# Attention: the maxima subtracted on strips of 32 rows with the four banks by turns, or on all 128 rows bank by bank

## The chip, the cores and the metric

One core of a Trainium2 chip runs the whole program. The metric is the device time of one execution in microseconds, as the median of the runs.

## The reference

The reference is one decoder block on x of 32 sequences x 128 tokens x 256: a selective scan, a cross attention with a context of the same shape, and a mixture of experts, each added to its input and followed by a normalisation without gain. The change touches the attention alone, cut to what matters:

```python
Q = query @ Wq.T; K = key @ Wk.T; V = value @ Wv.T
Q = _layernorm(Q, ln_gamma, ln_beta)      # over all 256, then 16 heads of 16
K = _layernorm(K, ln_gamma, ln_beta)
scores = jnp.einsum('bhqd,bhkd->bhqk', Q, K) / np.sqrt(D_K)
attn = jax.nn.softmax(scores, axis=-1)
context = jnp.einsum('bhqk,bhkd->bhqd', attn, V)
return context @ Wo.T
x = _layernorm(x + attention, axis=-1)
```

## The kernel before, in words

The program has five stages, each a block that all engines leave together: the scan, the attention, the choice of tokens by the experts, the experts, and the final normalisation.

The attention handles one sequence of 128 tokens at a time, as a pipeline written out by hand. One pass of the loop works on five sequences at once: it loads and splits the context of a sequence some passes ahead, projects sequence b+4 (query, key, value), normalises and transposes b+3, computes scores, maxima and exponentials of b+2, mixes the values of b+1 and projects them out, and normalises and stores b. The order of the work on each engine is the order of the calls in its function step; semaphores tie the engines together. The loop body holds two passes (even and odd buffers); the first eight passes and the last few are written out.

On TensorE (PE) a pass has this order: scores (b+2), mix_values first half (b+1), turn_x2 (b), mix_values second half, gates, turn_qk, project_kv first half, turn_top, shifted_scores first half, turn_x1, shifted_scores second half, subtract_top, project_kv second half, project_out, project_q.

The scores are computed twice. The first time (scores, L807) they are products of bf16 halves, only to find a maximum for each head and row: DVE reduces the four banks (maximum, L1032) into top, PE transposes it (turn_top, L815) and ACT copies it to topT in bf16 (copy_top, L947). The second time (shifted_scores, L825) they are products of split fp32 parts, transposed, with keys on the partitions. Then subtract_top (L835) adds minus the maximum to each column by a product of pick, which holds -1 in one row for each head and 0 elsewhere, with topT. Then ACT takes the exponential of each of the four banks (exps, L953), which waits for st_ready, counted once for each bank.

The 16 heads lie so that strip j (partitions 32j to 32j+31) holds heads 2j, 2j+1, 8+2j and 9+2j, and bank s_ps[j] holds the 4 x 128 columns of these four heads. topT has the maxima of strip j's heads in rows 32j to 32j+3, and pick has its -1 in the same strip: the other 96 rows of pick are 0 for that head. The products of scores and shifted_scores work on strips of 32 rows, strip j into bank j, j running innermost; those of subtract_top work on all 128 rows, one bank after another.

Of the kernel before, what the change touches and what calls it, by code (L numbers as in the profile page):

```python
# [17 lines left out]
P = 128  # L18
BATCH, SEQ, D = 32, 128, 256
T = BATCH * SEQ  # L20
KH = D // P
# [557 lines left out]
def attention_phase(nc, x1, ident, gate_all, const, ctxT_dram, table_dram, acc_dram, choice, row, row_stored, finished):  # L579

    with ExitStack() as ctx:
        s = Scope(nc, ctx, "attn")
        (q_w_hi, q_w_lo), (kv_w_hi, kv_w_lo), (o_w_hi, o_w_lo) = const.w_parts
        w_g, norm, affine, pick, eps, ident_bf = const.w_g, const.norm, const.affine, const.pick, const.eps, const.ident_bf
# [23 lines left out]
        topT = s.sb("topT", [P, P], BF16)  # L608
# [17 lines left out]
        s_ps = [s.ps(f"s{j}", [P, 512]) for j in range(4)]  # L626
# [7 lines left out]
        m = {n: s.sem(n) for n in names}  # L634
# [21 lines left out]
        with nc.Block() as block:  # L656
# [109 lines left out]
            def _(pe):  # L766
                def turn_x1(q):
                    pe.wait_ge(m["x1b_ready"], q.b + 1)
                    since(pe, m["x1T_ready"], q.b)
                    since(pe, m["top_ready"], q.b - 1)  # L770
                    for k in range(KH):
                        last = pe.transpose(turn_ps[:, k * P:(k + 1) * P], x1b[q.parity][:, k * P:(k + 1) * P], ident[:])
                    last.then_inc(m["x1_turned"], 1)
# [7 lines left out]
                def project_kv(q, k):  # L781
                    if k == 0:
                        pe.wait_ge(m["ctx_ready"], q.b + 1)
                        since(pe, m["v_ready"], q.b)
                    last = products(pe, kv_ps[:], [(ctx_hi[q.parity][:, k, :], ctx_lo[q.parity][:, k, :], kv_w_hi[:, k, :], kv_w_lo[:, k, :])],
                                    k == 0, k == KH - 1)
                    if k == KH - 1:
                        last.then_inc(m["kv_ready"], 1)

                def turn_qk(q):  # L790
                    pe.wait_ge(m["qkn_ready"], q.b + 1)
                    for i in range(2):
                        for k in range(KH):
                            c = (i * KH + k) * P
                            last = pe.transpose(q_ps[:, c:c + P], qkn[:, i, k * P:(k + 1) * P], ident[:])
                    last.then_inc(m["qkn_turned"], 1)

                def scores(q):

                    pe.wait_ge(m["qkb_ready"], 2 * (q.b + 1))  # L800
                    since(pe, m["exp_done"], 4 * q.b)
                    for k in range(KH):
                        for e in range(2):
                            c = (2 * k + e) * P
                            for j in range(4):
                                rows = slice(32 * j, 32 * j + 32)
                                last = pe.matmul(s_ps[j][:, c:c + P], qb[rows, k, e, :], kb[rows, k, :], start=True, stop=True)  # L807
                                if k == KH - 1 and e == 1:
                                    last.then_inc(m["s_ready"], 1)

                def turn_top(q):
                    pe.wait_ge(m["top_done"], 4 * (q.b + 1))
                    since(pe, m["g_exp_ready"], q.b - 1)
                    pe.wait_ge(m["x1T_ready"], capped(q.b + 2))
                    pe.transpose(turn_ps[:, 0:P // 2].bitcast(BF16), top[:].rearrange("p j h -> p (j h)"), ident_bf[:]).then_inc(m["top_turned"], 1)  # L815

                def shifted_scores(q, k):

                    if k == 0:
                        pe.wait_ge(m["top_done"], 4 * (q.b + 1))  # L820
                        pe.wait_ge(m["qk_low"], 2 * (q.b + 1))
                    for n, (kx, qx) in enumerate(((k_hi, q_hi), (k_hi, q_lo), (k_lo, q_hi))):
                        for j in range(4):
                            rows = slice(32 * j, 32 * j + 32)
                            pe.matmul(s_ps[j][:, 2 * k * P:2 * (k + 1) * P], kx[q.parity][rows, k, :],  # L825
                                      qx[q.parity][rows, k, :, :].rearrange("p e t -> p (e t)"),
                                      start=(k == 0 and n == 0), stop=False, skip_group_check=True)

                def subtract_top(q, j):
                    if j == 0:  # L830
                        pe.wait_ge(m["top_ready"], q.b + 1)
                    for k in range(KH):
                        for e in range(2):
                            c = (2 * k + e) * P
                            last = pe.matmul(s_ps[j][:, c:c + P], pick[:, 8 * k + 2 * j + e, :], topT[:], start=False, stop=True,  # L835
                                             skip_group_check=True)
                    last.then_inc(m["st_ready"], 1)

                def mix_values(q, k):

                    if k == 0:
                        since(pe, m["res_ready"], q.b)
                        pe.wait_ge(m["v_ready"], q.b + 1)
                        pe.wait_ge(m["exp_done"], 4 * (q.b + 1))
                    for e in range(2):
                        for n in range(2):
                            c = (KH * n + k) * P
                            for j in range(4):
                                value = vz[q.parity][:, 4 * k + j, 2 * e:2 * e + 2, :] if n == 0 else one_z[:, 2 * e:2 * e + 2, :]
                                last = pe.matmul(o_ps[32 * j:32 * j + 32, c:c + P], value.rearrange("p s d -> p (s d)"),  # L850
                                                 prob[q.parity][:, 4 * j + 2 * k + e, :], start=(k == 0 and e == 0 and n == 0),
                                                 stop=(e == 1), skip_group_check=True)
                    if k == KH - 1:
                        last.then_inc(m["pv_done"], 1)
# [6 lines left out]
                def turn_x2(q):  # L861
                    pe.wait_ge(m["x2_ready"], q.b + 1)
                    pe.wait_ge(m["x1T_ready"], capped(q.b + 4))
                    since(pe, m["g_exp_ready"], q.b)
                    for k in range(KH):
                        last = pe.transpose(turn_ps[:, (KH + k) * P:(KH + k + 1) * P], row[q.parity][:, k * P:(k + 1) * P], ident[:])
                    last.then_inc(m["x2_turned"], 1)

                def gates(q):
                    pe.wait_ge(m["x2T_ready"], q.b + 1)  # L870
                    for k in range(KH):
                        last = pe.matmul(turn_ps[:, 0:EXPERTS], x2T[:, k * P:(k + 1) * P], w_g[:, k, :], start=(k == 0), stop=(k == KH - 1))
                    last.then_inc(m["g_ready"], 1)

                def step(q, live):
                    if 2 in live:
                        scores(q.plus(2))
                    if 1 in live:
                        mix_values(q.plus(1), 0)
                    if 0 in live:  # L880
                        turn_x2(q)
                    if 1 in live:
                        mix_values(q.plus(1), 1)
                    if 0 in live:
                        gates(q)
                    if 3 in live:
                        turn_qk(q.plus(3))
                    if 4 in live:
                        project_kv(q.plus(4), 0)
                    if 2 in live:  # L890
                        turn_top(q.plus(2))
                        shifted_scores(q.plus(2), 0)
                    if 4 in live:
                        turn_x1(q.plus(4))
                    if 2 in live:
                        shifted_scores(q.plus(2), 1)
                        for j in range(4):
                            subtract_top(q.plus(2), j)
                    if 4 in live:
                        project_kv(q.plus(4), 1)  # L900
                    if 1 in live:
                        project_out(q.plus(1))
                    if 4 in live:
                        project_q(q.plus(4))

                pe.wait_ge(const.ready, const.steps)
                passes(pe, step)

            @block.scalar
# [973 lines left out]
```

## Time and profile before

| | us |
|---|---|
| median of 3 runs | 1446.86 |
| lowest and highest | 1442.95, 1447.52 |
| the profiled execution | 1447.94 |
| its span | 1446.1 |
| scan, to about | 535 |
| attention, to about | 893 |
| choice and experts, to about | 1380 |
| final stage, to | 1446 |

Times in the rows are microseconds from the start of the span. A timeline row merges instructions of one group that follow one another (xN); its first number is the start of the first, its second the time to the end of the last. In brackets stands the idle time of the engine before it and what ended it. PE is matmul, PEld its weight load. PEclk is the share of full clock granted to TensorE. The ends of matmuls are modelled, so distances are taken from start to start.

### The profile page before, as it was taken

The numbers are of one execution on the slowest core, as the hardware profiler recorded it, in microseconds if no ns is written. First come the engines' busy times: TensorE is split into PE (matmuls) and PEld (weight loads), VectorE is DVE, ScalarE is ACT, GpSimd is POOL, SyncE is SP. The second block draws the span as 40 slices with busy tenths as digits, with TensorE's granted clock in tenths as the row PEclk, the third lists the DMA queues.
The fourth block names the chain that finished last, engine by engine and source line by source line (L and its number), as shares of the span: only waits on it lengthen the run. The fifth ranks groups of instructions, "written<-read, shape, count | busy, mean of one in ns | idle before, by whom it ended". The sixth has DMA issues, their size and how long they took to land. (4 is left out here: it accounts for less than half of the span.)

```text
span 1446.1 us, 25901 instructions
## 1 busy us (share of the span) xinstructions
PE 1104.2 (76%) x8527; PEld 762.4 (53%) x8527; DVE 1019.3 (70%) x1875; ACT 748.1 (52%) x1605; POOL 805.4 (56%) x720
## 2 busy tenths in 40 slices
PE   5877778777787758888888886122999999999940
PEld 1322323222232237666676664022899899999940
DVE  2999999999999946677767765784455555555423
ACT  4666566575666436555666563100555555555425
POOL 2677676767768636666766764335144554455230
PEclk8999999999999979999999998555999999999975
DMA  3000000000000010111111100103134443343235
GB/s 103 15 15 1 15 0 15 15 0 15 0 0 0 1 28 27 35 33 33 33 41 36 33 32 26 65 1 101 56 63 107 94 106 81 89 112 55 24 47 215
DMA packets 42311, 64.00 MB, mean 44 GB/s; under 512 B 8161, under 2 KB 34465, under 8 KB 39073
## 3 DMA queue, kind: packets, MB, share of 16 engines
q1 hardware_dynamic: 29376, 41.92, 8.9%
q0 software_dynamic: 12288, 17.05, 7.2%
q10 hardware_dynamic: 576, 4.19, 0.7%
q8 instruction: 33, 0.54, 0.2%
q14 instruction: 38, 0.30, 0.1%
HBM read 42.00 MB, written 21.14 MB: 44 GB/s over the span
## 5 line engine op out<-in xcount | busy, mean ns | idle before, releaser
L514 POOL TENSOR_TENSOR scan_hc<-scan_state,scan_c_sb 128x1024 f32<-128x1024 f32 x128 | 304.1, 2380 | 142.9 <-DVE scan_state L442 132.0
L442 DVE TENSOR_TENSOR_SCAN scan_state<-scan_decay,scan_drive_ps 128x512 f32<-128x512 f32 x256 | 297.4, 1203 | 0.2
L223 PE MATMUL scan_y_ps<-scan_hc,all_ident 128*128 128x512 f32 x520 | 254.7, 613 | 2.1 <-POOL scan_hc L514 2.1
L1660 DVE TENSOR_TENSOR expert_hid_lo<-expert_hid,expert_hid_hi 128x512 fp32r<-128x512 f32 x128 | 88.5, 692 | 177.4 <-ACT expert_hid_hi L1644 165.7
L1557 POOL DMA_INDIRECT acc<-expert_rows,expert_lst x64 | 112.8, 1763 | 180.4 <-DVE expert_rows L1686 165.2
L1639 ACT ACTIVATE expert_hid<-expert_h_ps,expert_b 128x512 f32<-128x512 f32 x128 | 88.0, 688 | 200.0 <-PE expert_h_ps L556 191.9
L326 ACT ACTIVATE scan_decay<-scan_delta,scan_a_neg 128x508 f32<-128x508 f32 x256 | 169.2, 715 | 7.4 <-POOL scan_delta L496 7.2
L435 DVE TENSOR_TENSOR scan_drive_ps<-scan_dx,scan_b_ps 128x512 f32<-128x512 f32 x256 | 162.3, 679 | 14.6 <-POOL scan_dx L501 10.7
L368 ACT ACTIVATE scan_c_sb<-scan_c_ps 128x512 f32<-128x512 f32 x128 | 76.5, 598 | 138.2 <-PE scan_c_ps L216 129.2
L556 PE MATMUL expert_o_ps<-weights_w_hi,expert_hid_lo 128*128 128x256 f32 x512 | 143.4, 280 | 0.0
L554 PE MATMUL expert_o_ps<-weights_w_hi,expert_hid_hi 128*128 128x256 f32 x512 | 143.4, 280 | 0.0
L555 PE MATMUL expert_o_ps<-weights_w_lo,expert_hid_hi 128*128 128x256 f32 x512 | 143.0, 279 | 0.0
L223 PEld LDWEIGHTS scan_y_ps<-scan_hc,all_ident 128*128 128x128 f32 x520 | 98.9, 195 | 79.9 <-issue 71.9
L211 PE MATMUL scan_b_ps<-scan_bcs,scan_sel 96*128 96x512 bf16 x128 | 51.2, 400 | 115.1 <-DVE scan_drive_ps L435 115.1
L211 PEld LDWEIGHTS scan_b_ps<-scan_bcs,scan_sel 96*128 96x128 bf16 x128 | 12.4, 97 | 197.0 <-DVE scan_drive_ps L435 189.1
L554 PE MATMUL expert_h_ps<-expert_x_hi,weights_w_hi 128*128 128x512 f32 x256 | 106.1, 415 | 2.0 <-DVE expert_x_lo L1672 2.0
L556 PE MATMUL expert_h_ps<-expert_x_hi,weights_w_lo 128*128 128x512 f32 x256 | 102.1, 399 | 0.0
L555 PE MATMUL expert_h_ps<-expert_x_lo,weights_w_hi 128*128 128x512 f32 x256 | 102.1, 399 | 0.0
L554 PEld LDWEIGHTS expert_o_ps<-weights_w_hi,expert_hid_hi 128*128 128x128 f32 x512 | 96.0, 188 | 5.8
L555 PEld LDWEIGHTS expert_o_ps<-weights_w_lo,expert_hid_hi 128*128 128x128 f32 x512 | 96.0, 188 | 5.8
L556 PEld LDWEIGHTS expert_o_ps<-weights_w_hi,expert_hid_lo 128*128 128x128 f32 x512 | 96.2, 188 | 0.0
L1032 DVE TENSOR_REDUCE attn_top<-attn_s_ps 128x4 bf16<-128x512 f32 x128 | 83.4, 674 | 0.0
(226 smaller groups left out, 2543.5 us busy)
## 6 DMA issues: line engine op xcount, KB each, us to landing
weights_w<-w SPq DMA_DIRECT2D x16, 1024.0 KB
table<-all_row SPq DMA_DIRECT2D x32, 132.0 KB, 1.8
scan_xT<-xT SPq DMA_DIRECT2D x8, 512.0 KB, 3.9
attn_ctxT<-ctxT SPq DMA_DIRECT2D x32, 128.0 KB, 2.4
acc<-all_row SPq DMA_DIRECT2D x32, 128.0 KB, 1.7
final_a<-acc SPq DMA_DIRECT2D x4, 1024.0 KB, 7.2
out<-final_o ACTq DMA_DIRECT2D x4, 1024.0 KB, 5.8
expert_b<-b SPq DMA_DIRECT2D x8, 128.0 KB
```

What stands on the lines that cost most here:

```text
L223: last = pe.matmul(y_ps[k][:], ident[0][:], hc[:, n % RING, k, :], start=False, stop=(n == NS - 1))
L326: act.activation(decay[:, n % RING, k, :, 1:SEQ], delta[par][:, k, :, 1:SEQ], ACT.Exp, scale=a_neg[:, k, n:n + 1]).then_inc(decay_ready, 1)
L435: dve.tensor_tensor(drive_ps[k][:], dx[par][:, k, :], b_ps[:], ALU.mult).then_inc(drive_ready, 1)
L442: dve.tensor_tensor_scan(state[:, n % RING, k, :], decay[:, n % RING, k, :, :].rearrange("p b t -> p (b t)"), drive_ps[k][:], 0.0, ALU.mul ...
L514: pool.tensor_tensor(hc[:, n % RING, :, :], state[:, n % RING, :, :], c_sb[:, n % RING, :].unsqueeze(1).broadcast_to([P, KH, GT]), ALU.mul ...
L554: pe.matmul(out, a_hi, b_hi, start=start and n == 0, stop=False, skip_group_check=True)
L555: pe.matmul(out, a_hi, b_lo, start=False, stop=False, skip_group_check=True)
L556: last = pe.matmul(out, a_lo, b_hi, start=False, stop=stop and n == len(pairs) - 1, skip_group_check=True)
L1032: dve.tensor_reduce(top[:, j, 0:4], s_ps[j][:].rearrange("p (h k) -> p h k", k=P), AX.X, ALU.max).then_inc(m["top_done"], 1)
L1557: pool.indirect_dma_start(out=acc_dram, out_offset=bass.IndirectOffsetOnAxis(ap=lst[h.parity][:, n:n + 1], axis=0), in_=rows[h.part][:, t, ...
L1639: act.activation(hid[:, f % 2, :], h_ps[f % 2][:], ACT.Gelu, bias=b1[h.parity][:, f:f + 1]).then_inc(gelu_done, 1)
L1660: dve.tensor_tensor(hid_lo[:, f % RING_H, :], hid[:, f % 2, :], hid_hi[:, f % RING_H, :].bitcast(F32), ALU.subtract).then_inc(hid_ready, 1)
```

## The change

The function subtract_top takes all four banks in one call. Its loop over banks j becomes the innermost one, and each product takes only the 32 rows of strip j of pick and topT, which are the ones that are not zero for bank j. Four successive products then lie on four different strips and go to four different banks. The signals to ACT, one for each bank, now come with the last four products, where before each came with the fourth product of its bank. Number of products, their columns and their results are the same.

```diff
--- before.py
+++ after.py
@@ -826,15 +826,18 @@
                                       qx[q.parity][rows, k, :, :].rearrange("p e t -> p (e t)"),
                                       start=(k == 0 and n == 0), stop=False, skip_group_check=True)
 
-                def subtract_top(q, j):
-                    if j == 0:
-                        pe.wait_ge(m["top_ready"], q.b + 1)
+                def subtract_top(q):
+
+                    pe.wait_ge(m["top_ready"], q.b + 1)
                     for k in range(KH):
                         for e in range(2):
                             c = (2 * k + e) * P
-                            last = pe.matmul(s_ps[j][:, c:c + P], pick[:, 8 * k + 2 * j + e, :], topT[:], start=False, stop=True,
-                                             skip_group_check=True)
-                    last.then_inc(m["st_ready"], 1)
+                            for j in range(4):
+                                rows = slice(32 * j, 32 * j + 32)
+                                last = pe.matmul(s_ps[j][:, c:c + P], pick[rows, 8 * k + 2 * j + e, :], topT[rows, :], start=False, stop=True,
+                                                 skip_group_check=True)
+                                if k == KH - 1 and e == 1:
+                                    last.then_inc(m["st_ready"], 1)
 
                 def mix_values(q, k):
 
@@ -894,8 +897,7 @@
                         turn_x1(q.plus(4))
                     if 2 in live:
                         shifted_scores(q.plus(2), 1)
-                        for j in range(4):
-                            subtract_top(q.plus(2), j)
+                        subtract_top(q.plus(2))
                     if 4 in live:
                         project_kv(q.plus(4), 1)
                     if 1 in live:
```

## Rows read from the trace of the kernel before

**Rows 1.** the page, busy time of each engine, share of the span, instructions
```profile
PE 1104.2 (76%) x8527; PEld 762.4 (53%) x8527; DVE 1019.3 (70%) x1875; ACT 748.1 (52%) x1605; POOL 805.4 (56%) x720
```

**Rows 2.** windows, the attention stage: busy us (instructions) of PE, PEld, DVE, ACT, POOL; PEclk
```profile
535.00:893.00 358.00, 304.23 (x4753) 241.64 (x4752) 249.95 (x558) 210.35 (x621) 233.93 (x370) 0.95 0.10 33
```

**Rows 3.** timeline of PE in one pass: start us, us, engine, line, out<-in, count
```profile
707.03 0.44 PE L866 MATMUL attn_turn_ps<-all_ident,all_row 128*128 128x128 f32 x2 [1.22 <-POOL all_row L722]
...
711.50 0.28 PE L825 MATMUL attn_s_ps<-attn_q_hi,attn_k_lo 32*128 32x256 f32 x4
...
711.71 1.07 PE L835 MATMUL attn_s_ps<-attn_topT,xattn_pick 128*128 128x128 bf16 x16
...
712.59 0.47 PE L554 MATMUL attn_kv_ps<-xattn_w_kv_hi,attn_ctx_hi 128*128 128x512 f32 x1
...
713.95 0.28 PE L556 MATMUL attn_o_ps<-xattn_w_o_hi,attn_mixT_lo 128*128 128x256 f32 x1
...
715.04 0.40 PE L807 MATMUL attn_s_ps<-attn_kb,attn_qb 32*128 32x128 bf16 x16
```

**Rows 4.** timeline from project_out to turn_x2, and the waits of the whole stage
```profile
715.74 0.29 ACT L958 ACTIVATE attn_o_lnv<-attn_o_mv,xattn_eps 128x1 f32<-128x1 f32 x1 [0.76 <-DVE attn_o_mv L1053]
...
716.64 1.22 POOL L722 TENSOR_SCALAR all_row<-attn_res,attn_o_mv,attn_o_rstd 128x256 f32<-128x256 f32 x1 [2.34 <-ACT attn_o_rstd L961]
...
718.09 0.43 PE L866 MATMUL attn_turn_ps<-all_ident,all_row 128*128 128x128 f32 x2 [1.64 <-POOL all_row L722]
...
PE attn_turn_ps L866 <- POOL all_row L722: 44.9, 31, 1.8
```

**Rows 5.** timeline of PE: shifted products one behind another, products of scores, their neighbours
```profile
710.43 0.28 PE L825 MATMUL attn_s_ps<-attn_q_lo,attn_k_hi 32*128 32x256 f32 x4
...
710.55 0.28 PE L825 MATMUL attn_s_ps<-attn_q_hi,attn_k_lo 32*128 32x256 f32 x4
...
710.81 0.41 PE L772 MATMUL attn_turn_ps<-all_ident,attn_x1b 128*128 128x128 f32 x2
...
715.03 0.23 PEld L807 LDWEIGHTS attn_s_ps<-attn_kb,attn_qb 32*128 32x128 bf16 x16 [0.31 <-ACT attn_prob L953]
...
715.37 0.43 PE L850 MATMUL attn_o_ps<-attn_prob,attn_vz 128*32 128x128 f32 x8
```

**Rows 6.** timeline of ACT in that pass: the copy of the maxima, the four exps
```profile
710.39 0.28 ACT L947 ACTIVATE attn_topT<-attn_turn_ps 128x128 bf16<-128x128 bf16 x1 [0.92 <-PE attn_turn_ps L815]
...
712.88 2.10 ACT L953 ACTIVATE attn_prob<-attn_s_ps 128x512 f32<-128x512 f32 x4
```

**Rows 7.** timeline of PE at the first subtract_top and in the last passes
```profile
542.91 1.89 PE L835 MATMUL attn_s_ps<-attn_topT,xattn_pick 128*128 128x128 bf16 x16
...
544.56 0.78 PE L554 MATMUL attn_kv_ps<-xattn_w_kv_hi,attn_ctx_hi 128*128 128x512 f32 x1
...
872.66 0.44 PE L866 MATMUL attn_turn_ps<-all_ident,all_row 128*128 128x128 f32 x2 [1.15 <-POOL all_row L722]
...
878.01 0.38 PE L554 MATMUL attn_o_ps<-xattn_w_o_hi,attn_mixT_hi 128*128 128x256 f32 x1 [0.66 <-POOL attn_mixT_lo L733]
...
882.39 0.44 PE L866 MATMUL attn_turn_ps<-all_ident,all_row 128*128 128x128 f32 x2 [1.28 <-POOL all_row L722]
...
888.31 0.47 PE L554 MATMUL attn_o_ps<-xattn_w_o_hi,attn_mixT_hi 128*128 128x256 f32 x1
```

**Rows 8.** windows with the clock (behind the last bracket) down, then two passes
```profile
537.00:547.00 10.00, 9.05 (x58) 7.26 (x59) 2.94 (x6) 5.09 (x13) 5.59 (x10) 0.50 0.05 16
...
742.00:745.00 3.00, 3.00 (x20) 2.13 (x18) 1.83 (x4) 0.96 (x5) 2.61 (x5) 0.50 0.03 9
...
886.00:888.00 2.00, 2.00 (x29) 1.78 (x23) 0.30 (x3) 0.64 (x2) 1.12 (x2) 0.50 0.37 124
...
696.29:707.03 10.74, 9.34 (x152) 7.44 (x152) 7.88 (x19) 6.74 (x20) 7.38 (x13) 1.00 0.12 37
...
739.89:752.08 12.19, 10.73 (x151) 8.46 (x151) 7.88 (x19) 6.74 (x20) 7.37 (x13) 0.86 0.10 33
```

## The prediction

> **What bounds the kernel now.** I read the page first. PE has the largest busy share, 76%, but DVE has 70% [rows 1], so no engine is full. The windows by stage say where this change lies: the attention stage takes 358 us of 1446, PE is busy in 304 of them, and ACT, DVE and POOL each in 210 to 250 [rows 2]. It is a loop over 32 sequences with a few passes of ramp, so what counts is its period and which wait closes it. The page's chain that ended last covers only the final stage and says nothing of it; the stages before join at block ends, so whatever the attention stage loses comes off the end.
>
> The timeline of one pass gives the ring. On PE, turn_x2 starts at 707.03 and PE then goes on in order with no long gap to the end of project_out, with the next turn_x2 at 718.09 [rows 3]. The 16 products of subtract_top are in that stretch: 711.71 to the next product at 712.59. From the last product of project_out (713.95) the ring leaves PE: residual and its statistics on DVE, Ln on ACT at 715.74, Exp, normalise on POOL 716.64 to 717.86, and back to turn_x2 at 718.09, for which PE sat idle 1.64 us [rows 4]. The passes alternate between 10.74 us (696.29 to 707.03) and 11.06 (707.03 to 718.09) [rows 3, 4, 8] (the loop body holds two passes; the longer one has the turn of the loop in it). PE idles 44.9 us for POOL in the 31 passes that have a turn_x2 [rows 4]. So an edit on PE between turn_x2 and project_out shortens the period one for one, and an edit between project_out and turn_x2 (project_q, scores, the first half of mix_values) would not. The change is in the first stretch.
>
> **What the change takes away.** Sixteen products over all 128 rows. From the last group of shifted_scores (711.50) to the first product of project_kv (712.59) is 1.09 us, of which 0.21 is before the first of the sixteen and 0.88 from there on, 55 ns each [rows 3]. Groups of four shifted products that follow one another directly are 0.12 us apart (710.43 and 710.55) [rows 5]: so 0.12 of the 0.21 is the group's own work, and 0.09 is the passage from strips of 32 rows to all 128 rows, which the changed kernel no longer has at this place.
>
> **What it puts in.** Sixteen products on strips, four in different strips and banks behind one another. The trace of before has the same form: the products of scores are 32 rows by 128 columns, bf16, in the same order, with the same four signals on the last four. They take 0.33 us from the first (715.04) to the start of mix_values (715.37) [rows 3, 5], and that 0.33 holds a passage to another shape of the array. Weight loading doesn't stand against it: the loads of those sixteen take 0.23 us in all, less than the products [rows 5]. The passage here is to all 128 rows, in fp32; between shifted_scores and turn_x1 (710.55 to 710.81) it makes 0.26 us out of 0.12, 0.14 more [rows 5]. I take 0.12 + 0.33 + 0.02 = 0.47 us for the stretch in place of 1.09, a gain of 0.62 a pass, since the row with the same form is the nearest there is. The bounds: at best the 0.33 holds a passage of 0.14 that isn't paid here, so 0.12 + 0.19 + 0.02 = 0.33 and a gain of 0.76; at worst the whole 0.33 and a further 0.14 of passage, 0.59 and a gain of 0.50.
>
> The Trainium skill (TensorE: Matmul & The Clock Gate, section "Wait — 56ns, not 53.3ns?") says that starts of matmuls are never closer than about 25 ns. By that the sixteen would take 0.40 us before any passage, and the gain would be some 0.1 a pass smaller, 3 us in all. The trace doesn't agree: sixteen in 0.33 us, passage included, is 21 ns each.
>
> **What it moves.** Bank 0 was ready for exps after four products, now all four banks are ready together at the end. Before: 711.71 + 4 x 0.055 and the drain of 0.2. Now the end of the block is about 711.6 + 0.2 + 0.2 = 712.0. ACT reaches the first exps only at 712.88, behind scale_qk and high_of_x1, without a wait [rows 6]. So the reordering costs nothing; its cover is 0.9 us. No wait is added, no DMA, nothing on the queues of SP or POOL; the one wait for topT moves nowhere, and topT is ready at 710.67 [rows 6].
>
> **What is late next.** Three things hang on ACT and DVE and do not come earlier with project_out. First, exps end at 714.98, 7.95 us after turn_x2, and then Ln of the residual idles 0.76 for its statistics [rows 4, 6]; with those 0.62 earlier, 0.14 of cover is left. Second, scores starts at 715.04, on the end of exps [rows 3, 6], and stays there; with mix_values behind it, it ends about 716.3, against a turn_x2 at 717.47. The maxima behind it on DVE slip by about 0.15 against the residual. Third, mixT: where project_out is seen to wait for POOL's low part of it, it starts 878.01 - 872.66 = 5.35 us after turn_x2 [rows 7]. In the full pass the last product of project_out starts 713.95 - 707.03 = 6.92 after turn_x2 [rows 3], its first five products at 0.12 earlier, so at 6.3; 0.62 less leaves 5.7, and the slip of the maxima still fits. So a full 0.62 is to be had, but two covers are thin.
>
> **The sum.** The ring with both neighbours is there for 29 of the 32 blocks: 29 x 0.62 = 18.0. The first block runs at half clock and takes 1.65 us [rows 7]; on strips, twice 0.21 plus the passage is about 0.55, and with the passage before it 1.2 are gained, since PE goes on without a wait into the next scores. The last block but one gains nothing: project_kv is not behind it, and project_out waits 0.66 for mixT until 878.01 [rows 7]. The last, again at half clock [rows 8], would gain 1.2, but mixT comes at 882.39 + 5.35 = 887.74 and project_out starts at 888.31, so 0.6. Sum 18.0 + 1.2 + 0.6 = 19.8 us.
>
> **The clock.** PE falls to 0.50, its lower level of 1.2 GHz, in seven stretches from the first subtract_top to the last; the first, one in between and the last stand in [rows 8]. Five lie between ramp and tail, four of which make a pass longer by a like amount and one by twice as much. A pass with a short dip takes 12.19 instead of 10.74, 1.4 us more [rows 8]; the five cost some 8.5 us (four of 1.4, one of 2.9). They begin after a turn_x2 (739.89, the clock down by 742), behind an idle stretch of PE of 1.2 to 1.6 us for POOL [rows 3, 4, 8]. In the changed kernel scores and mix_values stay tied to exps while turn_x2 comes 0.62 earlier, so this idle stretch shrinks to 0.6 to 1.0, and the rest of it lies before scores. The longest idle stretch gets shorter, so I take two dips fewer, 2.8 us; with a price anywhere from none left (-8.5) to two more (+2.8).
>
> The profiled execution took 1447.94 us (span 1446.1), 1.08 above the median 1446.86. 1447.94 - 19.8 - 2.8 = 1425.3, less 1.08 is 1424.3; I say 1424.
>
> **Rivals.**
> - The clock falls more often. PE's work per pass gets smaller by 0.62 us of dense products while its idle time in a pass stays the same, and the period changes, so that dips could come in every pass. For it: every dip began after a stretch of thin work, and PE is busy 9.34 us of 10.74 [rows 8]. Against it: the shorter single gap. At 1.4 us each, 14 more dips eat the gain; a dip in all 30 passes (25 more, +35, and none saved, +2.8) gives 1462. Chance 0.05.
> - Strips don't run beside one another, for a reason that the scores do not have (the banks here are accumulated into, not started). Then the block stays at 0.88 and only the 0.09 of passage goes: 29 x 0.09 = 2.6, so 1444. Against it: shifted_scores accumulates on strips too, four products of 256 columns in 0.12 [rows 5]. Chance 0.05.
> - A cover is thinner than I read: ACT's Ln or the maxima close the ring after about 0.4 a pass. 29 x 0.4 + 1.8 = 13.4, no clock gain: 1433.5. For it: 0.14 us is left. Chance 0.13.
> - The dips between ramp and tail vanish: 5.7 more, 1418. Chance 0.15.
> - The forecast, 1424, has 0.60; 0.02 is left for what I don't see.
>
> The range: down to 1414 (no dips, -5.7, and the gain of 0.76 a pass, -4.1), up to 1436 (0.50 a pass, +3.5, and two dips more than now; this takes in the thin cover). About 0.3% (4.3 us) is what a measurement of this kernel tells from no change. Faster 0.89 (forecast, thin cover, no dips), same 0.06 (no concurrency), slower 0.05 (clock).
>
> **What would show it.** In a pass at full clock: 0.12 from the last shifted group to the block, then 0.33 to 0.37 to project_kv; sixteen busy about 0.4. Periods of 10.1 and 10.4. ACT idle before Ln about 0.1 in place of 0.76, PE idle for POOL under 1.0, scores directly on the end of exps with 0.5 to 0.9 idle before it. The attention stage about 337 us in place of 358, all other stages as now. Wrong would be: a block over 0.5, an idle stretch before turn_x2 that is still 1.6 us (then another wait has closed the ring), or ten or more dips.

## The result, and the profile after

The changed kernel takes 1422.1 us (median of 4 runs, 1418.9 to 1424.4) against 1446.0 for the kernel before beside it; the ratio is 0.9836, 95% interval 0.9806 to 0.9865. Forecast were 1424 and a range from 1414 to 1436. The profiled execution took 1419.96 us with a span of 1418.2.

The page and the windows by stage (busy us and number of instructions of PE, PEld, DVE, ACT, POOL; then PEclk, DMA share, GB/s) answer to [rows 1, 2]:

```profile
PE 1075.7 (76%) x8527; PEld 735.1 (52%) x8527; DVE 1020.1 (72%) x1875; ACT 748.8 (53%) x1605; POOL 805.2 (57%) x720
```

```profile
535.00:866.00 331.00, 281.82 (x4752) 216.39 (x4756) 248.09 (x554) 210.78 (x621) 232.81 (x368) 0.97 0.11 36
```

PE is busy 28.5 us less, its weight loads (PEld) 27 us less, and the other engines are busy as before. The attention stage is 331 us long in place of 358 (1.8 us of that is a scan that ended earlier), and its mean clock rose from 0.95 to 0.97. One pass, the short one of a pair, answers to [rows 3 to 6]:

```profile
684.89 0.29 PE L825 MATMUL attn_s_ps<-attn_q_hi,attn_k_lo 32*128 32x256 f32 x4
...
685.01 0.41 PE L837 MATMUL attn_s_ps<-attn_topT,xattn_pick 32*128 32x128 bf16 x16
...
685.35 0.50 PE L554 MATMUL attn_kv_ps<-xattn_w_kv_hi,attn_ctx_hi 128*128 128x512 f32 x1
...
686.29 2.10 ACT L955 ACTIVATE attn_prob<-attn_s_ps 128x512 f32<-128x512 f32 x4
...
688.50 0.29 ACT L960 ACTIVATE attn_o_lnv<-attn_o_mv,xattn_eps 128x1 f32<-128x1 f32 x1
...
688.54 0.41 PE L807 MATMUL attn_s_ps<-attn_kb,attn_qb 32*128 32x128 bf16 x16 [0.61 <-ACT attn_prob L955]
...
688.95 0.69 DVE L1034 TENSOR_REDUCE attn_top<-attn_s_ps 128x4 bf16<-128x512 f32 x1 [0.17 <-PE attn_s_ps L807]
...
689.27 1.23 POOL L722 TENSOR_SCALAR all_row<-attn_res,attn_o_mv,attn_o_rstd 128x256 f32<-128x256 f32 x1 [1.55 <-ACT attn_o_rstd L963]
...
690.55 0.44 PE L869 MATMUL attn_turn_ps<-all_ident,all_row 128*128 128x128 f32 x2 [0.59 <-POOL all_row L722]
```

The block of 16 products goes from 685.01 to 685.35, 0.34 us; with the 0.12 of the group before it the stretch is 0.46, where it was 1.09 [rows 3]. Ln follows the end of exps (688.39) after 0.11, where it had waited 0.76 [rows 4]. PE now idles 0.61 before scores, which sits on the end of exps, and 0.59 before turn_x2 in the short pass and 1.04 in the long one, where it was 1.22 and 1.64. The maximum on DVE now waits 0.17 for the scores. And the residual on DVE, which in the kernel before waited for project_out, now follows statistics_k without idle time; first the kernel before, then the changed one:

```profile
714.44 0.42 DVE L1045 TENSOR_TENSOR attn_res<-attn_o_ps,front_x 128x256 f32<-128x256 f32 x1 [0.45 <-PE attn_o_ps L556]
```

```profile
686.82 0.42 DVE L1010 BATCH_NORM_STATS2 attn_k_stats<-attn_kv_ps 128x6 f32<-128x256 f32 x1
687.24 0.42 DVE L1047 TENSOR_TENSOR attn_res<-attn_o_ps,front_x 128x256 f32<-128x256 f32 x1
```

Two successive passes, from turn_x2 to turn_x2, and the clock over most of the stage:

```profile
680.42:690.55 10.13, 8.93 (x152) 6.90 (x152) 7.74 (x19) 6.75 (x20) 7.40 (x13) 1.00 0.12 39
690.55:701.02 10.47, 8.91 (x151) 6.79 (x152) 8.28 (x19) 6.75 (x20) 7.74 (x13) 1.00 0.12 38
```

```profile
580.00:850.00 270.00, 232.82 (x3967) 178.62 (x3965) 209.59 (x472) 178.57 (x529) 196.63 (x312) 1.00 0.12 38
```

10.13 and 10.47 us in place of 10.74 and 11.06 [rows 3, 4, 8]. The clock doesn't fall once between 580 and 850; before, there were five dips between ramp and tail (the first passes and the last few). The traces of two more executions with the same passes, of the runs e1 and e12 below, show no dip between 580 and 845 either.

Where the 27.9 us between the two spans come from, read from the starts of the blocks: from the second block to the thirtieth, 553.26 to 866.74 before and 550.57 to 838.90 after, the stage is 25.15 us shorter. That is 28 passes. The dips were worth some 8.5 of it, which leaves 16.6, or 0.59 a pass. The first block gives 0.9, the last two 0.9, and the scan ended 1.8 earlier, which has nothing to do with the change; behind the last block 0.8 is lost.

### The profile page after: what moved, and what is told of

It reads as the page before. It is cut to its first block and busy times, and to the rows that moved or that the text cites. A ratio compares the mean times of both kernels' runs of the same rounds, so it can differ in the third digit from the quotient of the medians.

```text
span 1418.2 us, 25901 instructions
## 1 busy us (share of the span) xinstructions
PE 1075.7 (76%) x8527; PEld 735.1 (52%) x8527; DVE 1020.1 (72%) x1875; ACT 748.8 (53%) x1605; POOL 805.2 (57%) x720
```

## Experiments

Theory: a product on 32 rows leaves the other three strips free, and four strips run beside one another, so the block costs a quarter; and PE between turn_x2 and project_out closed the ring, so that each 0.1 us there is 0.1 us of a pass. Rivals: fewer rows are cheaper by themselves; the order of the banks does it; another link closes the ring. A second question is the clock: do the dips go because the idle stretch before turn_x2 got shorter?

**Strips, but bank by bank.** In the loop of the kernel before (the operands of the product alone are shown):

```diff
-  pick[:, 8 * k + 2 * j + e, :], topT[:]
+  pick[32 * j:32 * j + 32, 8 * k + 2 * j + e, :], topT[32 * j:32 * j + 32, :]
```

> The 16 products of subtract_top take only their 32 rows, but still bank by bank, so that four products in a row lie on the same strip. Theory (the gain comes from four strips working beside one another): the 16 stay 55 ns apart, the block stays near 0.88 us, and only the passage of 0.1 us between shifted_scores and the block is gone: passes of 10.6 and 11.0 us, about 3 us less than before, 1443. Rival (fewer rows are cheaper by themselves): the block falls to about 0.35 us and the time to about 1422.

Measured: 1422.25 us, ratio 0.9846 (0.9813 to 0.9879), as fast as the changed kernel. Its PE timeline:

```profile
683.80 0.29 PE L825 MATMUL attn_s_ps<-attn_q_hi,attn_k_lo 32*128 32x256 f32 x4
683.92 0.43 PE L835 MATMUL attn_s_ps<-attn_topT,xattn_pick 32*128 32x128 bf16 x16
684.28 0.51 PE L554 MATMUL attn_kv_ps<-xattn_w_kv_hi,attn_ctx_hi 128*128 128x512 f32 x1
```

The block is 0.36 us, not 0.88. So my theory was wrong in one point: the order of issue hardly matters at this size (0.02 us). Four products in a row on one strip don't hold up the ones behind them, which lie on another. The trace's records say so directly. The products start in four rounds of four, some 12 ns apart within a round and the rounds 55 to 67 ns apart. The program signals with its 4th, 8th, 12th and 16th product; by the records these four are the last four to start, in all 32 blocks of this run (in the kernel before they start 4th, 8th, 12th and 16th). So a product that is issued later, on another strip, starts ahead of an earlier one that waits for its own strip. By the time alone this run can't tell whether the strips overlap or whether 32 rows are cheap by themselves; the runs on one and two strips below do.

**Banks by turns, but all 128 rows.** In the changed kernel (operands alone):

```diff
-  pick[rows, 8 * k + 2 * j + e, :], topT[rows, :]
+  pick[:, 8 * k + 2 * j + e, :], topT[:]
```

> The banks by turns, but all 128 rows in each product. Theory: the block stays at 0.88 us with the passage before it, 1446 as before. Rival (writing four different banks in turn is what is fast): block near 0.35 us, 1422.

Measured: 1445.46 us, ratio 1.0002 (0.9983 to 1.0021).

```profile
699.93 0.29 PE L825 MATMUL attn_s_ps<-attn_q_hi,attn_k_lo 32*128 32x256 f32 x4
700.16 1.07 PE L837 MATMUL attn_s_ps<-attn_topT,xattn_pick 128*128 128x128 bf16 x16
701.03 0.48 PE L554 MATMUL attn_kv_ps<-xattn_w_kv_hi,attn_ctx_hi 128*128 128x512 f32 x1
```

0.87 us for the block and 0.23 before it; [rows 3] had 0.88 and 0.21. Turns without strips bring nothing; together with the run before, all of the gain belongs to the strips and none to the turns.

**One strip, two strips.** The block of the changed kernel with the strip and the bank taken modulo 1 or 2, all four exponentials behind the last product:

```diff
+  i = j % 1            # the other run: j % 2
-  rows = slice(32 * j, 32 * j + 32)
-  pe.matmul(s_ps[j][:, c:c + P], pick[rows, 8 * k + 2 * j + e, :], topT[rows, :], ...)
+  rows = slice(32 * i, 32 * i + 32)
+  pe.matmul(s_ps[i][:, c:c + P], pick[rows, 8 * k + 2 * i + e, :], topT[rows, :], ...)
```

> The changed kernel with all 16 products of subtract_top on one strip and one bank (the maxima of bank 0 are subtracted four times, those of the other banks not at all; all exponentials wait for the last product). The loads and the forms are those of the changed kernel, only the neighbouring strips are missing. Theory (strips run beside one another): 16 times 55 ns, a block of 0.88 us or a little more, passes near 10.65. Rival (a product of 32 rows costs less by itself): block 0.34.

> As the run on one strip, but strips 0 and 1 with banks 0 and 1 in turn, eight products each (their maxima are subtracted twice, those of banks 2 and 3 not at all). Theory: two side by side, 8 times 55 ns and the passage, a block of 0.55 us. Rival: 0.34.

Measured: 1452.17 us on one strip and 1432.12 on two (one run each). PE on one strip, then on two:

```profile
671.84 1.06 PE L838 MATMUL attn_s_ps<-attn_topT,xattn_pick 32*128 32x128 bf16 x16
672.84 0.50 PE L554 MATMUL attn_kv_ps<-xattn_w_kv_hi,attn_ctx_hi 128*128 128x512 f32 x1
```

```profile
669.18 0.63 PE L838 MATMUL attn_s_ps<-attn_topT,xattn_pick 32*128 32x128 bf16 x16
669.74 0.51 PE L554 MATMUL attn_kv_ps<-xattn_w_kv_hi,attn_ctx_hi 128*128 128x512 f32 x1
```

The block takes 1.00 us on one strip, 0.56 on two, 0.34 on four. The steps, 0.44 and 0.22, are eight and four times 55 ns: each strip takes its own products one by one at 55 ns, and the strips run beside one another. A product of 32 rows is no cheaper than one of 128. What is left over, 0.12, I take for the passage to the next shape; the last product on one strip starts 0.14 us ahead of project_kv, where the last one over 128 rows started 0.03 ahead. I had expected 0.88 "or a little more" on one strip and passes near 10.65, and had not added that passage; they are 10.77 and 11.12, so on one strip the change would have lost time. In these two runs the number of banks changes with the number of strips. Banks by turns gave nothing with 128 rows (the run before), but 32 rows on one strip into four banks, or on four strips into one bank, I did not run. With that left open, this settles the mechanism: strips beside one another, and not cheaper products.

**The strips' block twice.** The 16 products of the changed kernel are issued two times:

```diff
+  for k, e in [(k, e) for k in range(KH) for e in range(2)]:
+      for j in range(4):
+          pe.matmul(s_ps[j][:, c:c + P], pick[rows, 8 * k + 2 * j + e, :], topT[rows, :], start=False, stop=False, ...)
   (then the loops as they are)
```

> The changed kernel with the 16 products on strips issued twice (the maxima are subtracted twice). Theory (PE between turn_x2 and project_out closes the ring, one for one): block 0.22 us longer, passes of 10.34 and 10.70, 29 x 0.22 = 6.4 us more than the changed kernel, 1428.5. Rival (a cover has already closed the ring on ACT or DVE): the first part is hidden, passes stay near 10.12 and 10.48, 1422 to 1424.

Measured: 1432.21 us, ratio 0.9905 (0.9868 to 0.9942). PE in one pass, then windows of a whole pass and of two dips:

```profile
678.73 0.41 PE L836 MATMUL attn_s_ps<-attn_topT,xattn_pick 32*128 32x128 bf16 x16
678.97 0.40 PE L843 MATMUL attn_s_ps<-attn_topT,xattn_pick 32*128 32x128 bf16 x16
679.30 0.51 PE L554 MATMUL attn_kv_ps<-xattn_w_kv_hi,attn_ctx_hi 128*128 128x512 f32 x1
```

```profile
708.00:711.00 3.00, 3.00 (x21) 2.04 (x19) 1.84 (x4) 1.10 (x5) 2.63 (x5) 0.50 0.02 8
729.00:735.00 6.00, 6.00 (x57) 4.68 (x56) 3.45 (x6) 1.76 (x7) 4.22 (x7) 0.50 0.07 23
684.85:695.20 10.35, 8.95 (x168) 7.04 (x168) 7.79 (x19) 6.75 (x20) 7.39 (x13) 1.00 0.12 38
```

The block is 0.57 us, 0.23 more, and the pass 10.35 in place of 10.13: one for one, as forecast. PE still closes the ring in the changed kernel. The median rose by 10 us, not 6.4. In the profiled execution two dips are back, one of them long, which cost 4.4 us there; but that execution was the slowest of four (1435.73), so how much of the median they explain isn't known.

**No subtraction.** subtract_top is left out of the changed kernel, so the exponentials are taken of the raw scores; the last shifted products signal the banks (cut; the wait for topT now stands before the second half of the shifted products):

```diff
-  subtract_top(q.plus(2))
   (in shifted_scores, last group:)
+  if k == KH - 1 and n == 2:
+      last.then_inc(m["st_ready"], 1)
```

> The changed kernel without subtract_top: the exponentials are taken of the scores as they are, the last shifted products signal the banks. It asks how much cover is left. If PE still closes the ring, 0.34 us a pass is gained, 10 us, 1412. If exps and the Ln behind them close it after the 0.1 us of idle time that ACT has left before Ln, or mixT before project_out, only 0.1 to 0.15 a pass, 3 to 5 us, 1418. I expect the second; ACT idle before Ln is then zero.

Measured: 1422.2 us, ratio 0.9837 (0.9802 to 0.9872). ACT in two successive passes, the long one first, then the windows of both:

```profile
655.71 2.10 ACT L949 ACTIVATE attn_prob<-attn_s_ps 128x512 f32<-128x512 f32 x4
658.09 0.29 ACT L954 ACTIVATE attn_o_lnv<-attn_o_mv,xattn_eps 128x1 f32<-128x1 f32 x1 [0.28 <-DVE attn_o_mv L1049]
...
666.29 2.10 ACT L949 ACTIVATE attn_prob<-attn_s_ps 128x512 f32<-128x512 f32 x4
668.40 0.29 ACT L954 ACTIVATE attn_o_lnv<-attn_o_mv,xattn_eps 128x1 f32<-128x1 f32 x1
```

```profile
649.86:660.44 10.58, 8.83 (x136) 6.56 (x136) 8.41 (x20) 6.74 (x20) 7.74 (x13) 1.00 0.12 38
660.44:670.44 10.00, 8.74 (x135) 6.64 (x136) 7.41 (x19) 6.74 (x20) 7.38 (x13) 1.00 0.12 40
```

Not even the 3 us that I expected: the two passes together are 20.58 us against 20.60 in the changed kernel. The short pass is 0.13 us shorter. In it Ln follows exps (end 668.39) without any idle time, so there ACT closes the ring: turn_top, topT, scale_qk, exps, Ln. The long pass is 0.10 us longer. In it ACT still idles 0.28 before Ln, because project_out came late: it starts 0.48 after the last product of project_kv (655.11 and 655.59) where 0.23 is usual, just behind the end of mixT's low part on POOL (655.53). The change has taken nearly all that is to be had at this place; 0.34 us more of PE work taken away gives nothing.

**The gap filled, in the kernel before.** Six products into a part of turn_ps that turn_x2 overwrites, before its wait for POOL:

```diff
 def turn_x2(q):
-    pe.wait_ge(m["x2_ready"], q.b + 1)
     pe.wait_ge(m["x1T_ready"], capped(q.b + 4))
     since(pe, m["g_exp_ready"], q.b)
+    for n in range(6):
+        pe.matmul(turn_ps[:, KH * P:2 * KH * P], ident_bf[:], pick[:, 0:2, :].rearrange("p h q -> p (h q)"), start=True, stop=True)
+    pe.wait_ge(m["x2_ready"], q.b + 1)
```

> The kernel before, with six products of 128 rows and 256 columns put on PE where it would idle before turn_x2 (their result is overwritten by turn_x2). They take about 0.65 us of an idle stretch of 1.2 to 1.6, so the passes stay at 10.73 and 11.07 us. It asks whether the dips of the clock between ramp and tail come from that idle stretch. Theory: yes, the five dips of the kernel before are gone, and with them 8 us: 1437. Rival (they come with the length of the pass, or with anything but this gap): dips as before, 1445.

Measured: 1435.35 us, ratio 0.9929 (0.9907 to 0.995). The fillers and the gap behind them, then windows of this kernel and, last, of the kernel before over the same stretch:

```profile
719.07 0.83 PE L865 MATMUL attn_turn_ps<-xattn_pick,xattn_ident_bf 128*128 128x256 bf16 x6
720.36 0.44 PE L869 MATMUL attn_turn_ps<-all_ident,all_row 128*128 128x128 f32 x2 [0.46 <-POOL all_row L722]
```

```profile
709.62:720.36 10.74, 10.10 (x157) 7.94 (x158) 8.05 (x19) 6.74 (x20) 7.56 (x13) 1.00 0.12 37
720.36:731.25 10.89, 10.08 (x157) 7.92 (x158) 7.95 (x19) 6.74 (x20) 7.56 (x13) 1.00 0.11 37
```

```profile
550.00:880.00 330.00, 305.00 (x4779) 239.47 (x4777) 241.22 (x539) 203.87 (x603) 225.14 (x355) 1.00 0.11 35
```

```profile
550.00:880.00 330.00, 283.22 (x4446) 224.72 (x4446) 236.64 (x529) 200.16 (x592) 218.98 (x348) 0.97 0.11 34
```

Nothing is computed with these products, and the kernel is 10 us faster. The short pass is 10.74 as before, PE idles 0.46 where it was 1.22, and the clock is 1.00 throughout in place of 0.97. All six executions have a mean clock of 0.922 to 0.926, the seventeen of the kernel before beside them 0.912 to 0.921, so this is not the luck of one profile. The dips of the kernel before don't come from the length of the pass, then: the short one is unchanged. The fillers shorten an idle stretch and also add to PE's work (busy 10.10 us of a pass in place of 9.34), and this run can't tell the two apart. For the stretch speaks the changed kernel: it has no dips between 580 and 850, though PE is busy for nearly the same part of its short pass (8.93 us of 10.13, against 9.34 of 10.74). Nor is it a matter of that place alone. In the run with Ln ahead (below) PE doesn't idle before turn_x2 in the full passes, but 0.9 to 1.2 us before project_out and 1.2 before scores, and the clock still fell twice between 580 and 850, at 654 and 791. The long pass lost 0.17 besides (10.89 in place of 11.06), some 2 us in all. Why the turn of the loop costs less then, I did not find out.

**The gap filled, in the changed kernel.** The same edit with four products.

> The changed kernel with four products of 128 rows and 256 columns (0.43 us) put on PE where it idles before turn_x2 (0.59 or 1.04 us a pass; their result is overwritten by turn_x2). Theory (thin stretches before turn_x2 let the clock fall, and the changed kernel still has a dip or two in some executions, the ones with a mean clock of 0.913): the passes stay at 10.12 and 10.48, the slower executions near 1424 go, 1418 to 1420 with little spread. Rival (the dips of the changed kernel have another cause): 1422 with the same spread.

Measured: 1419.06 us (1417.1 to 1419.5 in five runs), ratio 0.9818 (0.9791 to 0.9844). Two passes:

```profile
700.87:710.98 10.11, 9.46 (x155) 7.18 (x156) 7.89 (x19) 6.74 (x20) 7.57 (x13) 1.00 0.12 39
710.98:721.28 10.30, 9.46 (x156) 7.10 (x156) 8.13 (x19) 6.74 (x20) 7.57 (x13) 1.00 0.12 39
```

**The changed kernel once more**, for its spread.

> The changed kernel once more, unaltered, for the spread of its executions beside the run with filled gaps (1419.06, from 1417.07 to 1419.45). Theory (filling the gaps takes dips out that the changed kernel has in some executions): its executions spread from about 1419 to 1424 with the lower mean clock in the slower ones, median near 1421.5. Rival (no difference): 1419, within 2 us.

Measured: 1420.05 us (1418.9 to 1431.5 in six runs), ratio 0.9849 (0.982 to 0.9877). Five of the six lie between 1418.9 and 1422.1; what the one at 1431.5 lost, no trace shows. The filled one has the best median of all kernels here and the smallest spread, and in the profile its long pass is 10.30 in place of 10.47, 14 times. From the first turn_x2 to the last it takes 316.8 us, where both profiled executions of the changed kernel take 319.2. But the intervals of the two ratios overlap: by the runs it is not clear that it is faster than the changed kernel.

**The second half of project_kv behind project_out.** In the step of PE:

```diff
-  if 4 in live: project_kv(q.plus(4), 1)
   if 1 in live: project_out(q.plus(1))
+  if 4 in live: project_kv(q.plus(4), 1)
```

> The changed kernel with the second half of project_kv moved behind project_out, out of the stretch of PE that closes the ring (0.8 us a pass). If PE alone closed the ring, 0.8 a pass would be gained, 23 us. I expect that the exponentials on ACT, with Ln right behind them, close it now, as in the run without subtraction: at most 0.1 to 0.15 a pass, 1418 to 1422, ACT idle before Ln zero, PE idle before turn_x2 or before scores larger by what PE no longer does there.

Measured: 1445.7 us, ratio 1.0002 (0.9987 to 1.0017), the whole gain lost. PE and DVE behind project_out:

```profile
675.34 0.28 PE L556 MATMUL attn_o_ps<-xattn_w_o_hi,attn_mixT_lo 128*128 128x256 f32 x1
...
675.93 0.39 PE L556 MATMUL attn_kv_ps<-xattn_w_kv_hi,attn_ctx_lo 128*128 128x512 f32 x1
...
676.36 0.43 DVE L1010 BATCH_NORM_STATS2 attn_k_stats<-attn_kv_ps 128x6 f32<-128x256 f32 x1 [0.59 <-PE attn_kv_ps L556]
...
676.71 0.41 DVE L1047 TENSOR_TENSOR attn_res<-attn_o_ps,front_x 128x256 f32<-128x256 f32 x1
```

The last product of project_out starts at 675.34, but residual (L1047) only at 676.71. DVE takes its work in order, and ahead of residual stands statistics_k (L1010), which now waits for the moved half of project_kv. I had looked at PE and ACT, not at DVE's queue. The passes at full clock are 10.58 and 11.01, half a microsecond longer than the changed kernel's, some 14 us. The rest of the loss goes at least in part with the clock, which fell eight times between 555 and 850 in the profiled execution, itself the slowest of eleven (1455.14).

**With DVE's statistics behind the residual too.**

```diff
   (DVE)
-  statistics_k(q.plus(4))
   residual(q.plus(1))
+  statistics_k(q.plus(4))
```

> As the run with the second half of project_kv behind project_out, and now DVE's statistics of the keys (statistics_k) behind the residual too, since before they stood ahead of it in DVE's queue and held the residual back until project_kv was done. Theory: with that the stretch of PE that closed the ring is 0.8 us shorter for good, but exps and the Ln right behind them on ACT close the ring after 0.1 us: passes of 10.0 and 10.4, ACT without idle time before Ln, 1419 at a full clock, and up to 10 us more where dips come with the longer idle time of PE. Rival (DVE's queue was not the reason): passes of 10.3 to 11, 1440 or more.

Measured: 1429.73 us, ratio 0.9897 (0.9864 to 0.9929). DVE's queue was a cause, as 16 us come back: the short pass is 10.13 again, the long one 10.94, together some 7 us, and in the profiled execution the clock fell once, in place of eight times. But my theory for what is left (passes of 10.0 and 10.4) was wrong as well. In a long pass:

```profile
701.25 0.38 PE L554 MATMUL attn_o_ps<-xattn_w_o_hi,attn_mixT_hi 128*128 128x256 f32 x1 [0.59 <-POOL attn_mixT_lo L733]
...
702.43 0.42 DVE L1047 TENSOR_TENSOR attn_res<-attn_o_ps,front_x 128x256 f32<-128x256 f32 x1 [0.31 <-PE attn_o_ps L556]
...
702.94 0.43 DVE L1010 BATCH_NORM_STATS2 attn_k_stats<-attn_kv_ps 128x6 f32<-128x256 f32 x1
...
703.43 0.43 DVE L1052 BATCH_NORM_STATS2 attn_o_stats<-attn_res 128x6 f32<-128x256 f32 x1
...
704.23 0.29 ACT L960 ACTIVATE attn_o_lnv<-attn_o_mv,xattn_eps 128x1 f32<-128x1 f32 x1 [0.62 <-DVE attn_o_mv L1055]
```

project_out idles 0.59 for mixT, the third of the covers, and the statistics of the residual (L1052) stand behind statistics_k, so that ACT still waits 0.62 before Ln. By these waits DVE and POOL close the ring in the long pass; no run takes them away to prove it. The kernel is slower than the changed one.

**Ln ahead of the last exps.** As before, with inv_std_o between the third and the fourth exps, moments_o on DVE right behind residual, and four fillers.

> As the run before it, and besides Ln and Exp of the residual on ACT before the last of the four exps, its statistics on DVE right behind the residual, and four filling products on PE before turn_x2. This takes the link from exps to Ln away. Theory: the ring is then closed by the maxima and the division on DVE on their way to mixT, or by scores and mix_values behind exps; passes of 9.6 to 10.0, 1405 to 1418. Rival: the moved Ln holds up the last exps and scores as much as it gains: 1420.

Measured: 1456.62 us, ratio 1.0079 (1.0052 to 1.0105), slower than the kernel before, with passes of 11.14 and 11.52:

```profile
699.69 1.62 ACT L958 ACTIVATE attn_prob<-attn_s_ps 128x512 f32<-128x512 f32 x3
702.45 0.29 ACT L963 ACTIVATE attn_o_lnv<-attn_o_mv,xattn_eps 128x1 f32<-128x1 f32 x1 [1.14 <-DVE attn_o_mv L1060]
...
702.88 0.58 ACT L958 ACTIVATE attn_prob<-attn_s_ps 128x512 f32<-128x512 f32 x1
```

ACT waits 1.14 us for the moments in the middle of exps, so that the last one ends at 703.46, 3.8 us after the first began in place of 2.1, and scores with all that follows waits for it. The rival had the right mechanism, but its 1420 was 37 us too low.

## Why the prediction was right

**What bounds the kernel**: the ring through PE between turn_x2 and project_out. Shown: taking 0.63 out gave 0.61 in the short pass and 0.59 in the long one, putting 0.23 in cost 0.22.

**The price of the new block**, 0.47 us for the stretch: measured 0.46. The row of scores, the same form in the same trace, was the right one to price it by. The rule of the Trainium skill (TensorE: Matmul & The Clock Gate, section "Wait — 56ns, not 53.3ns?") on starts no closer than about 25 ns, weighed there and set aside, doesn't hold here: 0.34 us for sixteen, passage included, and by the trace's records products on neighbouring strips start 5 to 7 ns apart.

**What it moves**: nothing was lost by signalling all banks at the end; ACT reached the exponentials 1.28 us after the start of the block, without a wait.

**The covers** (idle time of another engine that a gain on PE can use up): Ln idles 0.11 where 0.14 was read, scores sits on exps with 0.61 idle before it, the maxima slip by 0.17 where 0.15 was said. The rival of a thinner cover did not come, but the run without subtraction shows how near it was. The prediction's list of three was not complete. A fourth link is DVE's own queue, where the residual stands behind rest_of_x1 (the low part of the transposed x1, which waits for ACT) and statistics_k. Before, DVE idled 0.45 ahead of the residual, less than the 0.62 to be gained; now it idles nothing. The gain of 0.59 came all the same, because statistics_k, which waits for project_kv too, starts 0.13 earlier in the pass (6.40 after turn_x2 in place of 6.53): 0.13 and 0.45 are just enough. The residual still starts 0.49 after the last product of project_out, as before, so PE and DVE's queue now let it go at the same moment. That this link didn't cut the gain was luck; in the run with project_kv behind, the same queue cost the whole gain.

**The sum**: 19.8 forecast. Measured, without the clock and without the scan, are 16.6 for 28 passes, 0.9 for the first block and 0.9 for the end, 18.4, less 0.8 behind the last block. The terms that were a little too big are the pass, 0.59 for 0.62, and the first block, 0.9 for 1.2. The start of project_kv comes 0.63 earlier in the pass, but its second product follows the first after 0.34 us where it was 0.31 (685.35 and 685.69; 712.59 and 712.90), and the last product of project_out starts 6.33 after turn_x2 where it was 6.92: 0.59.

**The clock**: the direction came out as said, the size did not. I took two dips of five off; in the profiled execution all five are gone, 8.5 us and not 2.8. That is the rival with chance 0.15, for that execution. Two other executions of the changed kernel took 1424, and what they lost no trace shows: their mean clock was 0.913, but a third of the same kernel took 1418.9 at 0.917 without a dip between ramp and tail. That the shorter idle stretch is the reason is supported by the run with the gap filled, not proved by it.

**How near the number is** owes something to luck. Between the two profiled executions 22.6 us were forecast and 28.0 measured. The ring and its ends gave 17.6 in place of 19.8, the dips 5.7 more than said, and the scan 1.8 that nobody forecast. The first of these misses partly hides the other two. The forecast median then took 1.08 off, as the profiled execution before lay that far above its median; the profiled execution after lies 2.1 below its own. So by the medians, 1446.0 and 1422.1, the change is 23.9 us. The upper end of the range, 1436, is also more than the terms named for it give; those make 1433.

**A reading that fell**: I wrote of four products in different strips behind one another as if that order were needed. It isn't, here: bank by bank on strips is as fast. The Trainium skill (TensorE: Matmul & The Clock Gate, Part 3) says that matmuls start and end strictly in the order of the program. Then four in a row on one strip would have to hold back those behind them. The trace doesn't agree for the starts: 0.36 us for that order against 1.00 on one strip, and the four signalled products of the program's 4th, 8th, 12th and 16th place start last in all 32 blocks. The ends in the trace are modelled and show nothing of the order of ends.

## What to carry to other kernels

Here a product that used only one strip of 32 rows cost as much as a full one (55 ns), but four such on four strips and four banks cost one, and the passage to another shape of the array 0.12 us more; price it by a row of the same form. Before taking work out of one engine's stretch, list every link of the ring and its idle time, the order of each engine's own queue included: here the gain ended within about 0.1 us of the next link, and moving more work only found the queue that holds the next wait. An idle stretch of PE can cost a second time, if the clock falls behind it: filling it with products that nobody reads was worth 10 us in the kernel before.

## What the hardware showed that I had not expected

- Sixteen products of 32 rows and 128 columns, bf16, take 1.00, 0.56 and 0.34 us on one, two and four strips, with the passage to the next shape, and 0.36 when issued strip after strip. Products issued later, on another strip, start ahead of earlier ones that wait for their own strip.
- With PE's idle time before turn_x2 cut from 1.2 to 1.6 us down to 0.5 to 0.7 by products of no use, the clock of TensorE stayed at its upper level (2.4 GHz) for 330 us, at the same length of the short pass, where it had fallen to 1.2 GHz five times.
- The longer pass of each pair, the one with the turn of the loop, got 0.17 us shorter by the fillers in both kernels. The cause is open.
